# Turning the last query tile's probabilities by DMA transposes instead of by TensorE, in an attention and feed-forward block on one core

## The reference, cut to what matters

```python
def _L0_attn_ref(x, W_qk, W_v, alibi_slope):
    scores = jnp.einsum('bqe,bke->bqk', x @ W_qk, x) * SCALE
    scores = scores + (kpos - qpos) * alibi_slope[0]
    scores = jnp.where(qpos >= kpos, scores, -jnp.inf)
    attn = jax.nn.softmax(scores, axis=-1)
    v = x @ W_v.T
    return jnp.einsum('bqk,bkd->bqd', attn, v)

x = x + _L0_attn_ref(_layernorm(x), L0_attn_W_qk, L0_attn_W_v, L0_attn_alibi_slope)
x = x + _L0_ffn_ref(_layernorm(x), L0_ffn_w_gate, L0_ffn_w_up, L0_ffn_w_down)
```

## Time and profile before

| | |
|---|---|
| median of 3 runs | 143.6 us (143.3 to 144.7) |
| profiled execution, its own time | 143.12 us |
| profiled execution, span | 141.1 us |
| PE busy | 119.1 us (84% of the span) |
| DVE busy | 119.3 us (85%) |
| ACT busy | 109.4 us (78%) |
| POOL busy | 103.4 us (73%) |
| TensorE clock granted | full speed in all slices |

### The profile page before, as it was taken

The page is one execution under the profiler, slowest core; times in us unless marked ns, Lnnn a source line. Parts: engine busy times, 40 slices in busy tenths (PEclk is TensorE's granted clock), DMA queues, the critical chain, the costliest instruction groups (busy, mean ns, idle before and its releaser), DMA issues.

```text
span 141.1 us, 3405 instructions
## 1 busy us (share of the span) xinstructions
PE 119.1 (84%) x1183; PEld 88.1 (62%) x1183; DVE 119.3 (85%) x336; ACT 109.4 (78%) x249; POOL 103.4 (73%) x162
## 2 busy tenths in 40 slices
PE   0278578999999999889999998988994789979961
PEld 0066164768987869777869975667842545656661
DVE  0759989998788995989987969998869999998892
ACT  4035779999966999757999949977869689988920
POOL 6491789964992545996895999479669999995810
PEclk9999999999999999999999999999999999999999
DMA  4896000000000000000000001643001303057625
GB/s 133 230 255 177 3 2 2 5 2 0 5 0 0 5 0 2 0 5 0 0 5 0 5 0 40 99 89 79 0 5 37 79 0 79 6 73 213 198 78 153
DMA packets 18515, 7.28 MB, mean 52 GB/s; under 512 B 9152, under 2 KB 18496, under 8 KB 18496
## 3 DMA queue, kind: packets, MB, share of 16 engines
q1 hardware_dynamic: 18496, 7.02, 20.6%
HBM read 2.82 MB, written 2.10 MB: 35 GB/s over the span
## 4 chain that ended last, share of the span: by engine, by line
PE 32%; DVE 27%; POOL 14%; ACT 13%; DMA 5%; issue 5%; SPq 2%; DVEq 0%; POOLq 0%
DVE probsT_lo L805 5%; POOL hidden_lo L411 5%; PE work_ps L553 5%; PE attn_ps L566 3%; DVE biased L822 3%; DVE stats L707 3%; PE score_ps L501 3%; PE score_ps L503 3%; DMA x2T_lo<-xn_lo 3%; PE attn_ps L568 3%; PE attn_ps L567 3%; PE score_ps L502 3%; ACT probs L960 3%; ACT probsT_hi L982 2%; DVE xs L832 2%
## 5 line engine op out<-in xcount | busy, mean ns | idle before, releaser
L566 PE MATMUL attn_ps<-v_hi,probsT_hi 128*128 128x128 f16 x144 | 25.8, 219 | 2.4 <-DVE xs L832 1.7
L805 DVE TENSOR_TENSOR probsT_lo<-work_ps,probsT_hi 128x512 f16<-128x512 f32 (+3 forms) x48 | 25.2, 553 | 3.0 <-ACT probsT_hi L982 2.7
L960 ACT ACTIVATE probs<-biased,neg_max 128x128 f32<-128x128 f32 (+7 forms) x32 | 25.0, 783 | 3.2 <-DVE neg_max L822 3.1
L982 ACT CAST probsT_hi<-work_ps 128x512 f16<-128x512 f32 (+3 forms) x48 | 21.4, 483 | 6.4 <-PE work_ps L553 6.2
L822 DVE CUSTOM_DVE_ANT_0 biased<-score_ps,bias,neg_score_scale 128x128 f32<-128x128 f32 (+7 forms) x32 | 25.8, 806 | 0.6 <-PE score_ps L503 0.6
L568 PE MATMUL attn_ps<-v_hi,probsT_lo 128*128 128x128 f16 x144 | 25.8, 219 | 0.0
L567 PE MATMUL attn_ps<-v_lo,probsT_hi 128*128 128x128 f16 x144 | 25.7, 219 | 0.0
L553 PE MATMUL work_ps<-ident,probs 128*128 128x128 f32 x144 | 21.4, 274 | 1.3 <-DVE probsT_lo L805 0.7
L707 DVE BATCH_NORM_STATS2 stats<-xs 128x6 f32<-128x128 f32 x64 | 15.2, 283 | 5.2 <-DMA xs<-in_L_attn_x_dram 3.7
L553 PEld LDWEIGHTS work_ps<-ident,probs 128*128 128x128 f32 x144 | 16.5, 141 | 4.4 <-DVE probsT_lo L805 1.0
L566 PEld LDWEIGHTS attn_ps<-v_hi,probsT_hi 128*128 128x128 f16 x144 | 14.1, 98 | 5.5 <-DVE probsT_lo L805 1.8
(11 more groups left out here) (138 smaller groups left out, 331.5 us busy)
## 6 DMA issues: line engine op xcount, KB each, us to landing
out_dram<-xs SPq DMA_DIRECT2D x7, 256.0 KB, 3.2
xs<-in_L_attn_x_dram SPq DMA_DIRECT2D x3, 512.0 KB, 8.2
xs<-in_L_attn_x_dram SPq DMA_DIRECT2D x2, 256.0 KB, 3.1
out_dram<-xs SPq DMA_DIRECT2D x2, 128.0 KB, 2.0
wgu_int<-in_L_ffn_w_gate_dram SPq DMA_DIRECT2D x1, 192.0 KB, 3.0
wgu_int<-in_L_ffn_w_up_dram SPq DMA_DIRECT2D x1, 192.0 KB, 3.1
wd_int<-in_L_ffn_w_down_dram SPq DMA_DIRECT2D x1, 192.0 KB, 3.5
x2T_hi<-xn_hi SPq DMA_TRANSPOSE x8, 2.5
```

The lines of the kernel that those rows point to most:

```text
L566: pe.matmul(attn_ps[:, 0:D], p_hi, v_j, start=(j == 0), stop=False)
L805: dve.tensor_tensor(probsT_lo[:, i % 2, cols], work_ps[:, bank, 0:n], probsT_hi[:, i % 2, cols], ALU.subtract).then_inc(work_emptied, 1)
L960: act.activation(probs[:, i % 2, 0:n], biased[:, i % 2, 0:n], ACT.Exp, bias=neg_max[:, i:i + 1], scale=-1.0, accum_out=prob_sum[:, i:i + 1 ...
L982: act.copy(probsT_hi[:, i % 2, CW * h:CW * h + n], work_ps[:, bank, 0:n]).then_inc(probsT_hi_ready, 1)
```

## The change

For batches 0 to 2, the eighth query tile (`by_dma(b, i)`: i = 7 and b < 3) takes another way. Its exponentials go to a buffer of their own, `long_probs`. They stand at the end of round 4 on ACT, behind that round's copies, where they stood near the start of round 5. Two ACT copies then make the high part from `long_probs`, still untransposed, one for each 512 keys, and DVE makes the low part in round 5 (`split_long`). SP issues four DMA transposes: high and low part of the first half, high and low part of the second half. Each starts when its source is ready. PE no longer turns this tile (8 matmuls against the identity), ACT no longer copies and DVE no longer splits the turned tile from PSUM, and the ring loses two places per batch. `weigh_values` for this tile waits until all four transposes have landed. The fourth batch is as before.

```diff
+    def by_dma(b, i):
+        return i == TB - 1 and b < B - 1
...
-            if nb < B:
+            if nb < B and not by_dma(nb, ni):
                 ring += [("P", nb, ni, h) for h in range(ni // CT + 1)]
...
+            for b in range(B - 1):
+                if b:
+                    sp.wait_ge(attn_ready, TB * b)
+                for h in range(HALVES):
+                    for part, ready, o in ((long_hi, long_hi_ready, longT_hi), (long_lo, long_lo_ready, longT_lo)):
+                        sp.wait_ge(ready, HALVES * b + h + 1)
+                        sp.dma_start_transpose(o[:, CT * h:CT * (h + 1), :], part[:, CW * h:CW * (h + 1)])\
+                          .then_inc(longT_landed, 16)
             for n in range(B, NROUND):
...
             def transpose_probs(b, i):
+                if by_dma(b, i):
+                    return
...
             def weigh_values(b, par, i):
-                taken(("P", b, i, i // CT))
+                if by_dma(b, i):
+                    pe.wait_ge(longT_landed, 64 * (b + 1))
+                else:
+                    taken(("P", b, i, i // CT))
...
-                    p_hi, p_lo = probsT_hi[:, i % 2, keys], probsT_lo[:, i % 2, keys]
+                    if by_dma(b, i):
+                        p_hi, p_lo = longT_hi[:, j, :], longT_lo[:, j, :]
+                    else:
+                        p_hi, p_lo = probsT_hi[:, i % 2, keys], probsT_lo[:, i % 2, keys]
...
+            def split_long(b):
+                for h in range(HALVES):
+                    cols = slice(CW * h, CW * h + CW)
+                    dve.wait_ge(long_hi_ready, HALVES * b + h + 1)
+                    if b:
+                        dve.wait_ge(longT_landed, 64 * b)
+                    dve.tensor_tensor(long_lo[:, cols], long_probs[:, cols], long_hi[:, cols], ALU.subtract)\
+                       .then_inc(long_lo_ready, 1)
+
             def split_probsT(b, i):
+                if by_dma(b, i):
+                    return
...
                         bias_scores((i + 3) % TB)
+                    if i == 5 and by_dma(b, TB - 1):
+                        split_long(b)
                     if i + 1 < TB:
                         split_probsT(b, i + 1)
...
-                act.activation(probs[:, i % 2, 0:n], biased[:, i % 2, 0:n], ACT.Exp, bias=neg_max[:, i:i + 1],
+                if by_dma(b, i) and b:
+                    act.wait_ge(long_lo_ready, HALVES * b)
+                o = long_probs[:, 0:n] if by_dma(b, i) else probs[:, i % 2, 0:n]
+                act.activation(o, biased[:, i % 2, 0:n], ACT.Exp, bias=neg_max[:, i:i + 1],
...
+            def long_high(b):
+                act.wait_ge(probs_ready, TB * (b + 1))
+                if b:
+                    act.wait_ge(longT_landed, 64 * b)
+                for h in range(HALVES):
+                    cols = slice(CW * h, CW * h + CW)
+                    act.copy(long_hi[:, cols], long_probs[:, cols]).then_inc(long_hi_ready, 1)
+
             def copy_probsT(b, i):
+                if by_dma(b, i):
+                    return
...
                     if i + 2 < TB:
-                        exponentials(b, i + 2)
+                        if not by_dma(b, i + 2):
+                            exponentials(b, i + 2)
...
+                    if i == 4 and by_dma(b, TB - 1):
+                        exponentials(b, TB - 1)
+                        long_high(b)
```

More of the change, by code:

```diff
@@ L87, in emptied, with copied_probs @@
         return sum(by_pool(k) == by_pool(key) for k in ring[:ring_index[key] + 1])
+    def copied_probs(key):
+        return sum(k[0] == "P" for k in ring[:ring_index[key] + 1])
     VECTOR_TAKES, POOL_TAKES = (sum(by_pool(k) == who for k in ring) for who in (False, True))
@@ L240, in preln_block @@
         probs_ready = sem("probs_ready")
+        long_hi_ready = sem("long_hi_ready")
+        long_lo_ready = sem("long_lo_ready")
+        longT_landed = sem("longT_landed")
         attn_ready = sem("attn_ready")
```

7 lines of the change are left out of this document (6 added, 1 removed).

## The result

The changed kernel takes **151.31 us** (median of 4 runs, 151.06 to 151.58) against 143.53 us (4 runs, 143.3 to 144.7) for the kernel before: ratio **1.0525, 95% interval 1.0472 to 1.0578**. The forecast was 148.2 us with a range from 145.0 to 151.5. The direction is right and the time lies at the range's upper edge. The mechanism is only partly the one forecast, as the rows show. The profiled execution took 151.06 us with a span of 148.9 us.

A forecast was written before the change was run, and what follows sets the result against it. No single engine bounds; each batch ends at PE's weighting of tile 7. Late transposes add 1.7 + 0.8 + 1.7 = 4.2 us to 143.12, giving 147.3, or 148.8 with one slow landing; 148.2 us taken, range 145.0 to 151.5.

The forecast's parts named there:

- What bounds the kernel: Each batch ends at PE's weighting of tile 7; from there to the next batch's round 5 on ACT stays 13.40 us.
- ACT point: Where round 5 begins on ACT, at 34.27, 54.29 and 75.37 us before; the forecast counts each batch's delay from it.
- PE's relief of 3.3 us: PE no longer turns tile 7: at most 0.9 x 3 + 0.55 us saved, swallowed whole by PE's next wait.
- the landing: Last transpose lands 6.43 us after the first issue, delaying tile 7's weighting by 1.7, 0.8 and 1.7 us: +4.2 us.
- ACT, the first transpose 1.9 us behind the point: Exponentials 1.24, copy 0.62 and semaphore 0.03 us make the first high half ready 1.9 us after round 5's ACT start.
- SP, 1.31 us apart: SP issues the four transposes at its own pace of 1.31 us, the fourth 3.93 us after the first.
- DVE in rounds 5 and 6: Subtractions move ahead of tile 6's split: tile 5's addition about 1.0 us later, won back in round 6; no added cost.
- rival 3: Transposes hidden by faster, overlapping issue; DVE still sets each batch's end: 143.1 to 143.7 us, chance 0.11.
- idle time of 1 us or more at L599: Sign in the profile after: PE's first matmul of tile 7, batches 0 to 2, waits this long for DMA `longT_lo`.
- Contention on the subtractions: DVE's subtractions with two SBUF inputs slowed beside POOL in batch 2: +0.3 us, left in the range.

The follow-up runs named there:

- e5: The changed kernel with round 5's scaled sum moved back ahead of tile 7's exponentials on ACT: 149.47 us, ratio 1.0432.
- e6: The changed kernel with 18 filling transposes on PE ahead of the v projection and no wait for the landing (old probabilities multiplied): 147.93 us, ratio 1.0284.
- e1: The changed kernel without the wait for the four transposes, old probabilities of tile 5 multiplied for tile 7: 150.87 us, ratio 1.0519.
- e2: The changed kernel with 18 more f32 identity transposes on PE in round 6, ahead of the v projection: 152.62 us, ratio 1.0596.
- e4: The changed kernel with the two long copies at the end of round 5 and the two subtractions in round 6: 161.33 us, ratio 1.1203.
- e7: The changed kernel with long copies and subtractions one round later and no wait for the landing (old probabilities multiplied): 147.54 us, ratio 1.0244.
- e8: The changed kernel with two DMA transposes of 128x1024 per batch instead of four of 128x512: 149.85 and 150.59 us (two further runs 152.19, 152.24), ratio 1.0456.
- e9: The changed kernel with e8's transposes, scaled sum and tile 6's copies ahead of the long copies, tile 6's split ahead of the subtractions: 147.01 us, ratio 1.0212.
- e10: e9 with tile 7's weighting and addition moved into the next batch's round 0: 148.22 us, ratio 1.0337.

## Why the prediction was right, and where it was not

1. **What bounds the kernel.** Right. The stretch from the weighting of tile 7 to the next ACT point took 57.30 - 43.89 = 13.41 and 80.09 - 66.69 = 13.40 us, as in the kernel before, and each batch's delay went whole into the next. The distances between the weightings of tile 7 were 22.80 and 23.30 us, where 21.7 was forecast.
2. **PE's relief of 3.3 us is swallowed.** Right in that the kernel gained nothing by it. But it was set against the late bank, not against the landing: the first filling of round 6 came 2.29, 1.61 and 2.48 us late, and 1.07 us of that per batch came back since tile 7 was not turned. The 0.55 us that I read in the earlier trace rows as a wait for the exponentials, and counted as relief, was a wait for this very bank and not to be had. Seen rightly, it would have told that PE had no slack there.
3. **ACT, the first transpose 1.9 us behind the point.** Right: 36.95 - 35.03 = 1.92, 59.29 - 57.30 = 1.99, 82.06 - 80.09 = 1.97 us.
4. **SP, 1.31 us apart.** Right for the last pair, 1.31 us each time, and the middle one is 1.23. The second comes 1.82, 1.75 and 1.96 us behind the first instead, since its subtraction stands behind the reciprocal. With the measured landing of 2.5 us the last lands 8.8, 8.8 and 9.0 us behind the ACT point, not 8.33 (8.48 in batch 1): the landing term should have been +5.6 us, not +4.2.
5. **DVE in rounds 5 and 6, "0 to 0.2 us later per batch, and the landing covers that". This step failed.** I put the addition of tile 5 about 1.0 us later and let DVE win it back in round 6. It came 5.90 us behind the ACT point in batch 0 (40.93 - 35.03) against 3.62 (37.89 - 34.27), 2.28 us later. I had counted which instructions moved and their durations, but not that the reciprocal of round 5 waits for the scaled sum of 128x1, which the order rows ahead of the prediction show behind the long copies. So DVE stood idle and did the subtractions after that wait, not in it, and the split of tile 6 came 2.29, 1.62 and 2.50 us later. Nor had I counted that PE's first filling of round 6 waits for that split, in both kernels, so that the lateness reaches PE before DVE can win it back. The scaled sum is the smaller part of that lateness: with it in front again (e5) PE still waits 1.28 to 2.19 us at the bank, behind the copies and the subtractions. By itself the order costs 4.3 us (e6). That it equals the 4.2 us forecast for the landing is chance.
6. **The clock** has no term in the prediction. I took full clock for granted because it had been full in the earlier trace rows. A PE idle for 2.2 to 2.4 us in one piece lost it in two batches of three: 2.9 us by e1 against e6.
7. **The landing**, forecast as the whole of it, is worth 0.4 us in the kernel as it stands (e1), 4.7 us once PE comes in time (e2 against e6), and 13.8 us when the copies come a round later (e4 against e7). In rival 3's terms, the transposes were hidden, but by a delay of the same size and not by speed. I had asked for idle time of 1 us or more at L599; it was 0.55 us once.
8. **Contention on the subtractions.** Small here, as taken: 0.68 to 0.91 us each. It counts in e7 and in batch 2 of e5.

The range held the time because its upper part was meant for slow landings and contention; what filled it was neither.

What stays open: why the clock fell in batches 1 and 2 of the changed kernel and in 0 and 1 of e1, after the same idle times; why single transposes land after 4 us instead of 2.5; and how the 4.3 us of the order divide between the scaled sum and the subtractions once clock and landing are out, for e5 has both in it.

## What to carry to other kernels

When a step moves in an in-order queue, look at the smallest instruction that it is moved past: a scaled sum of 128x1 held DVE for 2.26, 0.28 and 1.87 us, and putting it back gave 1.8 us, the clock's part included. Where buffers are used in a ring, work out which piece each filling waits for and how much slack it has: here it had next to none, and a late split passed to PE one for one. Where the profile names a releaser that had long been done, look for another; the 0.55 us put down to ACT would have pointed at this bank. Where several waits end within a microsecond of each other, taking one away shows nothing (0.4 us here); take them away in pairs, for the same landing wait was worth 4.7 us once the first was filled.

## What the runs showed of the hardware

- A DMA transpose between SBUF buffers took SP 1.19 to 1.34 us per instruction, for 128x512 and for 128x1024 f16 alike, but for single ones of 1.44 us (e5), 1.81 us (e6) and 2.06 us (e2). It landed after 2.4 to 2.6 us (128x512, changed kernel) and 3.1 to 3.4 us (128x1024; e8, e9, e10). The slowest of 128x512 took 4.0 to 4.6 us (e2, e4, e6, e7).
- The granted clock fell behind idle stretches of PE, or within them, and not each time: with waits of 2.2 to 2.4 us it fell to 0.50 for some 3.4 us in two batches of three (changed kernel; two of three in e1 too), with 1.3 to 2.2 us in one of three (e5), and with waits of 4.3 and 6.3 us it was there for 6.8 us in each batch (e4). The length of the wait does not decide alone: in e9 the clock fell in batch 1 with a wait of 1.69 us and held in batch 2 with 1.91 us. With the gap filled by matmuls it held (e6).
- Two f32 subtractions of 128x512 with both inputs in SBUF took 1.3 us on DVE beside POOL work on 128x8 (changed kernel, batch 0; e7, batch 2) and 2.1 to 2.5 us beside POOL's arithmetic of 128x512 (e5, batch 2; e7, batches 0 and 1), against 1.15 to 1.28 us with one input in PSUM (kernel before).
